# Expert tiles without filling: 32 dense tiles of tokens, cut into 39 pieces of tile and expert

## What is computed

```python
flat = layernorm(x).reshape(-1, 512)                       # N = 2048 tokens
shared_out = (sigmoid(flat @ shared_gate.T) * (flat @ shared_up.T)) @ shared_down.T
weights = softmax(flat @ router_w.T)                       # 8 experts
top_w, top_idx = top_k(weights, 2)                         # every token picks 2
he = sigmoid(xb @ wg[e].T) * (xb @ wu[e].T)                # bfloat16, 352 wide
routed = sum over the 2 picks of top_w * (he @ wd[e].T)
x = x + flat + shared_out + routed                         # as the block returns it
```

## Time and profile before

| what | us |
|---|---|
| three timed executions | 655.4, 659.87, 660.19 (median 659.87) |
| the profiled execution | 653.7, its span 651.7 |
| PE busy | 606.6 (93% of the span), 4110 matmuls |
| DVE busy | 507.6 (78%) |
| ACT busy | 472.0 (72%) |
| POOL busy | 360.0 (55%) |
| granted clock of PE | 0.995 of full speed over the span |

### The profile page before, as it was taken

How to read it: one execution, slowest core, us unless ns; L and a number is a source line. 1 busy time by engine, 2 the same in 40 slices (tenths; PEclk the granted TensorE clock), 3 DMA queues, 4 the chain that set the end, 5 groups by cost and what they waited for, 6 DMA issues and landing times.

```text
span 651.7 us, 12576 instructions
## 1 busy us (share of the span) xinstructions
PE 606.6 (93%) x4110; PEld 259.2 (40%) x4110; DVE 507.6 (78%) x970; ACT 472.0 (72%) x662; POOL 360.0 (55%) x494
## 2 busy tenths in 40 slices
PE   4799999999999999999999999879999999999987
PEld 4543333333333333333333332224554466666532
DVE  2479899999999999999999999964528654454577
ACT  3654899899899899899898888985432276667511
POOL 5559453684684684684684462251553577777310
PEclk9899999999999999999999999999999999999999
DMA  8642434534525535534433432115698533333178
GB/s 293 195 135 76 114 93 145 168 110 144 170 87 168 167 89 171 167 112 146 135 111 102 132 111 80 50 52 121 170 220 184 110 105 106 100 106 107 50 230 310
DMA packets 64990, 88.66 MB, mean 136 GB/s; under 512 B 12624, under 2 KB 45264, under 8 KB 63904
## 3 DMA queue, kind: packets, MB, share of 16 engines
q1 hardware_dynamic: 60032, 68.72, 34.4%
q0 software_dynamic: 4896, 19.14, 12.1%
HBM read 63.75 MB, written 32.74 MB: 148 GB/s over the span
## 4 chain that ended last, share of the span: by engine, by line
PE 76%; DVE 11%; issue 6%; ACT 5%; DMA 1%; POOL 1%; SPq 0%; ACTq 0%; DVEq 0%; POOLq 0%
PE PS L1083 17%; PE PS L986 11%; PE PS L1311 9%; PE PS L1055 8%; PE PS L1774 7%; DVE MX L996 7%; PE PS L845 5%; PE PS L1837 4%; PE PS L1585 4%; ACT E L1069 2%; PE PS L840 2%; PE PS L991 1%; PE PS L933 1%; PE PS L1732 1%; PE PS L929 1%
## 5 line engine op out<-in xcount | busy, mean ns | idle before, releaser
L996 DVE TENSOR_REDUCE MX<-PS 128x1 f32<-128x512 f32 x512 | 323.1, 683 | 17.3 <-PE PS L986 15.4
L1069 ACT ACTIVATE E<-PS 128x1024 f32<-128x1024 f32 x256 | 253.5, 1020 | 32.7 <-PE PS L1055 28.6
L986 PE MATMUL PS<-BIG 53*128 53x512 f16 x512 | 128.6, 384 | 12.2 <-DVE MX L996 10.8
L1083 PE MATMUL PS<-E,BIG 128*32 128x512 f32 x1024 | 136.4, 605 | 2.0 <-ACT E L1069 2.0
L1055 PE MATMUL PS<-BIG 55*128 55x512 f16 x512 | 101.2, 381 | 8.2 <-ACT E L1069 3.5
L879 POOL TENSOR_TENSOR ML<-BIG,ML 128x512 f32<-128x512 f32 x30 | 38.3, 1277 | 102.8 <-ACT BIG L855 102.6
L986 PEld LDWEIGHTS PS<-BIG 53*128 53x128 f16 x512 | 34.3, 93 | 134.0 <-DVE MX L996 120.1
L1796 DVE SCALAR_TENSOR_TENSOR E<-WP,PS 128x352 bf16<-128x352 f32 x39 | 20.3, 521 | 47.0 <-ACT WP L1786 47.0
L1774 PE MATMUL PS<-BIG,CT 128*128 x312 | 53.0, 313 | 1.8 <-DVE WP L1346 1.0
L855 ACT ACTIVATE BIG<-PS,BIG 128x256 f32<-128x256 f32 x64 | 35.7, 560 | 25.9 <-PE PS L840 14.5
L1856 POOL DMA_INDIRECT scr_ys<-SW,bvB x39 | 38.3, 981 | 20.8 <-DVE SW L1849 12.5
(11 more groups left out here) (261 smaller groups left out, 904.0 us busy)
## 6 DMA issues: line engine op xcount, KB each, us to landing
scr_parts<-WP SPq DMA_DIRECT2D x96, 128.0 KB
BIG<-scr_parts SPq DMA_DIRECT2D x64, 192.0 KB
BIG<-in_we POOLq DMA_DIRECT2D x8, 1088.0 KB, 14.1
scr_u<-ML SPq DMA_DIRECT2D x32, 256.0 KB, 3.0
X<-in_x SPq DMA_DIRECT2D x8, 512.0 KB, 6.5
CT<-in_ctx SPq DMA_DIRECT2D x8, 512.0 KB, 4.1
ML<-scr_u SPq DMA_DIRECT2D x16, 256.0 KB
ML<-scr_recs SPq DMA_DIRECT2D x16, 256.0 KB
```

What stands on the lines that cost most here:

```text
L986: e.matmul(PS[:, yi[name] % 3, :], QK[rows, qb(u), 0, j0 + jj, 128 * tt:128 * tt + 128], QK[rows, qb(u), 1, j0 + jj, :], start=True, stop= ...
L996: e.tensor_reduce(MX[:, g % 2, c:c + 1], PS[:, yi[name] % 3, :], AX.X, ALU.max)\
L1069: e.activation(E[:, st, 2 * jj:2 * jj + 2, :], PS[:, slot(name):slot(name) + 2, :], ACT.Exp, scale=1 / 1024).then_inc(s["rc"], 1)
L1083: ins = e.matmul(PS[32 * hh:32 * hh + 32, AVB, :], VT[:, b % 2, st, 4 * (g % 4) + hh, :], E[:, st, hh, :], start=(st == 0), stop=(st == 3))
```

## The change

The slots are now counted without rounding: expert e's pairs begin where those of expert e-1 end (`PO`, with 1.0 in place of 128.0), so that 4096 pairs fill 32 tiles exactly. A tile can hold pairs of several experts. Work is cut into pieces, each of one tile and one expert; there are at most 32 + 7 = 39, and always 39 are computed. A piece passes the whole tile through its expert's weights, and a mask with 0.5 in the rows of that expert and 0 elsewhere multiplies the result, which is added to the tile's rows in `YS`.

- `turn_slots` and `gather_slots` run for 16 pairs in place of 20, and the indirect stores for 32 tiles in place of 39. The number of pieces through `gate_up`, `turn_hidden` and `down` stays 39.
- `XT` has 10 tile slots in place of 4, in the space of the shared expert's first weights; `gate_up` reads which slot from a second register, so both operands of its matmuls have offsets from registers, and `reg_load` fills 16 registers at a time in place of 8.
- `YS` has 16 tiles. DVE clears each before its first use (`clear`, 32 memsets of 128x256 words), and the scaling becomes a masked addition at an offset from a register, with 8 registers loaded on DVE every 8 pieces.
- The tables for this are made on DVE: `owners` grows, `pieces`, `segments` and `masks` are new; the steps `weights` and `places` move behind the first pieces.
- The first pair's copy to `XT` waits for the last G; the first register load stands behind the first transposes.

```diff
-        XT = [cf[:, 2048 + 1024 * i:3072 + 1024 * i].rearrange("p (k n) -> p k n", k=4) for i in range(2)]
-        YS = [free[:, 1024 * i:1024 * i + 1024].rearrange("p (a n) -> p a n", a=2) for i in range(4)]
+        XT = swh[:, 0:5120].bitcast(BF)
+        YS = E[:, 2:4, :, :].rearrange("p b k t -> p (b k t)").bitcast(BF)
...
-            dve.at(when(("G", 2, 1)) + .78 * dt_, weights)
+            dve.at(tb + 2., weights)
...
-                st(e, e.tensor_scalar(NI, PS[:, bank, 128:136], 127.0, None, ALU.add))
-                st(e, e.tensor_scalar(NI, NI, 7, None, ALU.logical_shift_right))
-                st(e, e.tensor_copy(TC, NI))
+                st(e, e.tensor_copy(TC, PS[:, bank, 128:136]))
                 inc = running(TC, I0, I1, 8)
                 st(e, e.tensor_tensor(BX, inc, TC, ALU.subtract))
-                st(e, e.scalar_tensor_tensor(PO, BX.rearrange("p (o a) -> p o a", o=1).broadcast_to([128, 16, 8]), 128.0,
+                st(e, e.scalar_tensor_tensor(PO, BX.rearrange("p (o a) -> p o a", o=1).broadcast_to([128, 16, 8]), 1.0,
...
+            def wide(v):
+                return v.rearrange("p (o a) -> p o a", o=1).broadcast_to([128, NTILE, 8])
+
             def owners(e):
+                st = dch.step
+                inc, running = runs
+                st(e, e.tensor_copy(NI, BX))
+                st(e, e.tensor_scalar(NI, NI, 7, None, ALU.logical_shift_right))
+                st(e, e.tensor_copy(FE, NI))
+                st(e, e.scalar_tensor_tensor(ME, FE, -128.0, BX, ALU.mult, ALU.add))
+                st(e, e.tensor_scalar(ME, ME, 0.5, None, ALU.is_gt))
+                st(e, e.scalar_tensor_tensor(XE, TC, 0.5, ME, ALU.is_gt, ALU.mult))
+                st(e, e.tensor_tensor(XI, running(XE, J0, J1, 8), XE, ALU.subtract))
+                st(e, e.tensor_tensor(XI, XI, ME, ALU.add))
+                st(e, e.tensor_tensor(SE, FE, XI, ALU.add))
+                st(e, e.tensor_tensor(CM, bc(iotaf[:, :], NTILE), wide(SE), ALU.is_ge))
+                st(e, e.tensor_reduce(EF, CM, AX.X, ALU.add))
+            dve.at(when(("G", 2, 1)) + .77 * dt_, owners)
+
+            def pieces(e):
+                st = dch.step
+                st(e, e.tensor_tensor(C2, CM, wide(XI), ALU.mult))
+                st(e, e.tensor_reduce(XL, C2, AX.X, ALU.max))
+                st(e, e.tensor_scalar(EOF[:, :, 0], EF, -1.0, 4352.0, ALU.add, ALU.mult))
+                st(e, e.tensor_tensor(TU, iotaf[:, :], XL, ALU.subtract))
+                st(e, e.tensor_scalar(TT, TU, NS - 1.0, None, ALU.min))
+                st(e, e.tensor_scalar(MA, TT, 9.5, -10.0, ALU.is_gt, ALU.mult))
+                st(e, e.tensor_tensor(MC, TT, MA, ALU.add))
+                st(e, e.tensor_scalar(MA, TT, 19.5, -10.0, ALU.is_gt, ALU.mult))
+                st(e, e.tensor_tensor(MC, MC, MA, ALU.add))
+                st(e, e.tensor_scalar(MA, TT, 29.5, -10.0, ALU.is_gt, ALU.mult))
+                st(e, e.tensor_tensor(MC, MC, MA, ALU.add))
+                e.tensor_scalar(EOF[:, :, 1], MC, 512.0, None, ALU.mult).then_inc(s["rt"], 1)
+            dve.at(when(("G", 3, 0)) + .725 * dt_, pieces)
+
+            def segments(e):
+                st = dch.step
                 inc = runs[0]
-                dch.step(e, e.tensor_tensor(CM, bc(iotaf[:, :], NTILE),
-                                            inc.rearrange("p (o a) -> p o a", o=1).broadcast_to([128, NTILE, 8]),
-                                            ALU.is_ge))
-                dch.step(e, e.tensor_reduce(EF, CM, AX.X, ALU.add))
-                e.tensor_scalar(ET[:, :], EF, 7.0, 4352.0, ALU.min, ALU.mult).then_inc(s["rt"], 1)
-            dve.at(when(("G", 2, 1)) + .77 * dt_, owners)
+                st(e, e.tensor_tensor(C2, CM, wide(BX), ALU.mult))
+                st(e, e.tensor_reduce(LO, C2, AX.X, ALU.max))
+                st(e, e.tensor_tensor(C2, CM, wide(inc), ALU.mult))
+                st(e, e.tensor_reduce(HI, C2, AX.X, ALU.max))
+            dve.at(when(("G", 3, 0)) + .73 * dt_, segments)
+
+            def masks(e):
+                st = dch.step
+                st(e, e.scalar_tensor_tensor(LO, TU, -128.0, LO, ALU.mult, ALU.add))
+                st(e, e.scalar_tensor_tensor(HI, TU, -128.0, HI, ALU.mult, ALU.add))
+                st(e, e.tensor_scalar(LO, LO, PCOL, 0.5, ALU.is_lt, ALU.mult))
+                st(e, e.scalar_tensor_tensor(MKI, HI, PCOL, LO, ALU.is_ge, ALU.mult))
+                st(e, e.tensor_scalar(MA, TT, 15.5, -16.0, ALU.is_gt, ALU.mult))
+                st(e, e.tensor_tensor(MC, TT, MA, ALU.add))
+                e.tensor_scalar(ETO, MC, 512.0, None, ALU.mult).then_inc(s["mk"], 1)
+            dve.at(tb + .38, masks)
...
-            dve.at(when(item) + .12 * dt_, places)
+                e.scalar_tensor_tensor(OX[:, :], IA, -1.0, IN, ALU.add, ALU.add).then_inc(s["ox"], 1)
...
-                if j == 4:
-                    e.wait_ge(s["gu"], len(gi))
                 if j >= 8:
                     e.wait_ge(s["xt"], j - 7)
-                for a in range(min(2, NTILE - 2 * j)):
+                for a in range(2):
...
+                o = 1024 * (j % 5)
                 if j == 0:
+                    e.wait_ge(s["gu"], len(gi))
                     e.wait_ge(s["xt0"], 1)
-                    e.activation(XT[0][:, :, 0:128], rows[:, :, 0:128], ACT.Copy).then_inc(s["xte0"], 1)
+                    e.activation(XT[:, 0:512], bank[:, 0:512], ACT.Copy).then_inc(s["xte0"], 1)
                     e.wait_ge(s["xt"], 1)
-                    e.activation(XT[0][:, :, 128:256], spare.rearrange("p (k n) -> p k n", k=4)[:, :, 128:256], ACT.Copy).then_inc(s["xte"], 1)
+                    e.activation(XT[:, 512:1024], spare[:, 512:1024], ACT.Copy).then_inc(s["xte"], 1)
                     return
                 e.wait_ge(s["xt"], j + 1)
-                if j >= 2:
-                    e.wait_ge(s["g2"], 2 * (j - 1))
-                e.activation(XT[j % 2], rows, ACT.Copy).then_inc(s["xte"], 1)
...
-                    if j:
+                    if 0 < j < NS // 2:
                         e.wait_ge(s["xte"], j + 1)
                     if j and j % 4 == 0:
                         n = min(8, NTILE - q)
-                        e.reg_load(regs[0:n], ET[0:1, q:q + n])
-                expert[q] = e.snap(regs[q % 8], min_val=0, max_val=7 * 4352)
+                        e.reg_load(regs[0:2 * n], ET[0:1, 2 * q:2 * q + 2 * n])
+                expert[q] = e.snap(regs[2 * (q % 8)], min_val=0, max_val=7 * 4352)
+                tile = e.snap(regs[2 * (q % 8) + 1], min_val=0, max_val=9 * 512)
                 for c in range(2):
                     for k in range(4):
-                        ins = e.matmul(PS[:, 2 * a + c, 0:352], XT[j % 2][:, k, 128 * a:128 * a + 128],
+                        ins = e.matmul(PS[:, 2 * a + c, 0:352], XT[:, bass.ds(tile + 128 * k, 128)],
                                        big[:, bass.ds(expert[q] + (1408 * c + 352 * k), 352)],
                                        start=(k == 0), stop=(k == 3))
                 ins.then_inc(s["g2"], 1)
...
+                    e.wait_ge(s["mk"], 1)
+                    held.extend(e.alloc_register(f"place{i}") for i in range(8))
+                if r % 8 == 0:
+                    n = min(8, NTILE - r)
+                    e.reg_load(held[0:n], ETO[0:1, r:r + n])
+                place = e.snap(held[r % 8], min_val=0, max_val=15 * 512)
+                if r:
+                    e.wait_ge(s["de2"], r)
+                if r < NS:
+                    e.wait_ge(s["zr"], r + 1)
+                e.wait_ge(s["d2"], r + 1)
+                e.scalar_tensor_tensor(YS[:, bass.ds(place, 512)], PS[:, 4 + a, :], MKI[:, r:r + 1], YS[:, bass.ds(place, 512)],
+                                       ALU.mult, ALU.add).then_inc(s["de2"], 1)
+
+            def clear(e):
+                if r == 0:
                     e.wait_ge(s["gu"], len(gi))
-                if j >= 4 and a == 0:
-                    e.wait_ge(s_ys[j % 4], 32 * (j // 4))
-                e.tensor_scalar(YS[j % 4][:, a, :], PS[:, 4 + a, :], 0.5, None, ALU.mult).then_inc(s["de2"], 1)
+                if r >= 16:
+                    e.wait_ge(s_ys[(r - 16) // 4], 64)
+                e.memset(YS[:, 512 * (r % 16):512 * (r % 16) + 512], 0.0).then_inc(s["zr"], 1)
+            if r < NS:
+                dve.at(tb + j + 1 + (.36 if a == 0 else .8), clear)
...
             def place(e):
-                if r == 0:
+                t = r - 7
+                if t == 0:
                     e.wait_ge(s["ox"], 1)
                 e.wait_ge(s["de2"], r + 1)
-                e.indirect_dma_start(ys, bass.IndirectOffsetOnAxis(ap=OX[:, r:r + 1], axis=0), YS[j % 4][:, a, :], None)\
-                    .then_inc(s_ys[j % 4], 16)
+                e.indirect_dma_start(ys, bass.IndirectOffsetOnAxis(ap=OX[:, t:t + 1], axis=0),
+                                     YS[:, 512 * (t % 16):512 * (t % 16) + 512], None).then_inc(s_ys[t // 4 % 4], 16)
```

(13 more changed lines are left out.)

66 lines of the change are left out of this document (36 added, 30 removed), and 2 rows, old and new, of the table s.

## The result

The changed kernel takes 665.31 us (median of four runs), the kernel before 659.69 beside it: ratio **1.014**, 95% interval 1.009 to 1.019. The ratios here are the ones on record for each set of runs and not quotients of the medians: these two medians are 5.6 us apart (1.0085), while the ratio says some 9 us, with executions of 655.4 to 660.19 us before and 662.84 to 669.96 after. Two further sets of runs gave 1.0126 [1.0072, 1.0181] and 1.0113 [1.0078, 1.0147]. The forecast was 661.5 us and no measurable change.

The account below looks back on a forecast made before the run. PE was taken to bound the expert stage (busy 96.02 of 97.63 us). Terms -1.8 + 2.7 + 1.5 + 0.1 = +2.5 us gave 662.4 on the median, put at 661.5 us; range 654.5 to 668.5.

Parts of the forecast that it names:

- x-turns, -1.8: PE, last pairs of the expert stage: tokens turned for 16 pairs in place of 20, 0.45 us each, 1.8 us off.
- Tables, +2.7: DVE ahead of and among the first pieces: the new tables delay hidden values and PE, +2.7 us (0 to +4.4).
- Loads on PE, +1.5: PE's register loads, four now of 16, 16, 16 and 14: +1.5 us exposed (0 to 3.5), the first hidden.
- Offsets on PE, 0: First 4 matmuls of each piece compute two addresses per instruction: 0 us, up to 3.3, as the sequencer can run ahead.
- memset and addition, 0.3 and 0.69: DVE in the steady part: memset 0.3 us and masked addition 0.69 us, covered by idle time before the next hidden values.
- PE kept up: Against the rival that PE's sequencer becomes the bound, +3.3 us with a doubled 46 ns, 665.5 us; chance 0.13.
- POOL and DVE didn't hold each other up: Against the rival that DVE's memsets and additions wait for POOL's indirect DMAs all stage, +14 us, 676; chance 0.09.
- DVE's own loads: DVE's register loads, 5 times about 0.7 us, partly beside the memset and just fitting; the last may cost a few tenths.
- Tail, +0.1: End of the kernel: the last tile is still stored after the last piece, so +0.1 us for tail and last load.

Follow-up runs that it names:

- after_again: The changed kernel run again with no edit, as the measure for the runs beside it; ratio 1.0126 to the kernel before.
- pe_by_pair: Changed kernel with PE loading four registers per pair, one pair ahead, in place of 16 every fourth pair; ratio 1.0061 to the kernel before.
- before_16_turns: Kernel before without the turns of x of its last four pairs (16 to 19), run on another chip; ratio 0.9987.
- rows_by_one: Changed kernel with DVE loading one row-offset register per piece, 39 loads, in place of eight at a time; ratio 1.0064 to the kernel before.

## Why the prediction was wrong

The time, 665.3, lies in the range; that it would be no measurable change does not hold. By its steps, against `after_again`, whose stage ran at the full clock:

- **x-turns, -1.8: three of the four.** The last two pairs have 4.02 us for 4.46, and in `pe_by_pair` the pair with the first missing turn 4.03. The pair between them, with a product of the shared expert, keeps its 6.42. Timeline of PE in that pair, first the kernel before, then `after_again`:

```profile
603.14 0.81 PE L1837 MATMUL PS<-BIG,XN 128*128 x3
603.79 1.46 PE L1585 MATMUL PS<-SW,WP 128*128 128x512 f16 x6
```

```profile
609.29 0.59 PE L1885 MATMUL PS<-BIG,XN 128*128 x2
610.11 1.47 PE L1633 MATMUL PS<-SW,WP 128*128 128x512 f16 x6 [0.23 <-DVE E L1905]
```

The product starts 2.23 us behind the start of the gate_up ahead of it (607.88), where it was 1.84 (601.95), because PE now waits for DVE's masked addition; that takes 0.39 of the 0.45 that the missing turn gave. `before_16_turns` has no such addition, and its pair fell to 5.97. The term was worth about -1.3.

- **Tables, +2.7: right in kind, 3.29 measured.** The hidden values of G(3,1) came 3.39 later where 3.1 stood, the first gate_up 2.35 where 1.4 stood. `pieces` ended 0.4 us later than I had it (526.77 less the 3.93, for 522.4), and the load behind it took 1.29 us where I had left 1.1.
- **Loads on PE, +1.5: right, about 1.7.** Smaller loads took 2.91 us off the changed kernel and 1.23 off the one before. The loads of the earlier trace rows were thus themselves a cost that I took as given. (They begin 0.8 us before PE runs dry, not 0.6.)
- **Offsets on PE, 0; memset and addition, 0.3 and 0.69: near.** Of the 273 instructions that compute offsets, 117 now took 74 to 83 ns in place of 46, and pairs without a load keep their 4.46 us, so PE kept up. Memset and addition take 0.27 and 0.75. POOL and DVE didn't hold each other up in this stage: all 32 memsets took 0.27 us and all 39 additions 0.74 to 0.75.
- **DVE's own loads, "5 times about 0.7, partly runs beside the memset and just fits": the step that failed.** They took 1.62 to 2.09 us and cost 2.97. The 0.7 came from PE's row with the same number of registers. The number was the same and the address was not: `ET` is the start of the tables and `ETO` their word 78, 8 bytes beside a multiple of 16. With that mended, the step comes true word for word (0.62, and it fits).
- **Tail, +0.1: right in the order of work** (32.37 for 32.36), but in other profiles it is longer by 1.3 to 3.0 us (33.66 to 35.33), with matmuls at the lower clock in each of them and a longer idle stretch in some (2.92 us in `rows_by_one`); my sum had no term for it.

Sum: 3.29 + 2.97 + 1.7 - 1.3 = 6.7 of 6.9 us. Of the 4.4 us by which the 6.86 go beyond my +2.5, DVE's loads are by far the largest part. What the ratios show beyond 6.9 (7.4 to 9.2 us) goes with the mean clock: the executions of the changed kernel in `after_again`'s set at 0.995 took 659.5 and 660.3 us, those at 0.987 and 0.990 took 665.8 and 664.5. The kernel before at 0.995 took 653.3 to 656.4 us beside them.

And the dense tiles themselves? With every load mended in both, the packed kernel is at 97.20 and the kernel before at 97.87 us; 0.9965 and 0.9958 can't be told apart. Of the 1.8 us for four turns 0.67 arrives: turn 2 still comes 0.24 later, the pair with the shared expert's product has 6.37 us (5.97 in `before_16_turns`), and the last pair 4.32 where it had 4.02 in `rows_by_one`. I found no gain beyond that in the change.
